# Rank-2 projection of the last pair over 128 rows, and a new order of the first stage, in a gated low-rank feed-forward kernel

## The chip, the cores and the metric

The kernel runs on one core of a Trainium2 chip. The metric is the device time of one execution in microseconds; the time before is 862.0 us, the median of three runs (861.14 to 862.42).

## The reference, cut to what matters

```python
def _qlora_linear(x, wq, A, B):          # wq holds a quarter of the input columns
    w = jnp.tile(wq, (1, 4))
    return x @ w.T + x @ A.T @ B.T * 0.5

def reference(x, w1q, a1, b1, w3q, a3, b3, w2q, a2, b2):     # x: 2 x 2048 x 1024
    xn = layernorm(x)
    s = attn(xn)        # autocorrelation by FFT, its top 6 lags, a softmax over them
    g = silu(_qlora_linear(silu(_qlora_linear(xn, w1q, a1, b1)) * _qlora_linear(xn, w3q, a3, b3),
                           w2q, a2, b2))                     # hidden width 2752, rank 2
    return x + s * g
```

## The kernel before

The 4096 tokens are done in eight groups of 512 (NG = 8), each of four tiles of 128 tokens. The normalised tile is folded to a quarter of its columns, since the weights repeat four times. Each fp32 product with the weights w1 and w3 is made as three fp16 products: the high part of the weights times the high part of x, high times low, and low times high. Hidden columns go by pairs: pair p is 128 columns of w1 (the gate, bank gb[p % 3]) and 128 of w3 (the factor beside it, bank ub[p % 3]). There are 22 pairs (NP_), and the last one (LAST = 21) holds 64 columns of each, side by side.

In a group, TensorE runs `up(i, p)` for each pair (`chain` makes the six products of a bank, L1223; `lora`, L1251, adds the rank-2 part for two pairs at once), ScalarE takes the silu (`gate`), and VectorE multiplies (`product`, L826), which gives h, a ring of six buffers. Every fourth pair TensorE projects four pairs of h onto the rank of a2: `z2(i, n)` (L1365) writes pair p to rows 32 * (p % 4) of the bank zb, so that the four pairs lie in four column strips of the array. The last call, n = 5, holds pairs 20 and 21 alone, and pair 21 reads 64 rows where all others read 128. After it come the second linear layer (`down`, L1424 to L1433, in group 0 `down_high` and `down_low`), the transposes of the next group's x (`xt_across`, L1455), and from group 1 to group 6 `z_across` (L1351), transposes of zs, which VectorE makes by `z_split` (L801) after the first output tile of the group.

All engines work from queues written out by hand, joined by semaphores; nothing is reordered at run time but the loading of weights into the array. The order in the source is the order of the work.

The first stage, before the first pair, differs from the others. SP loads the small a13, the identity, the tiles of x and the weights in four blocks (BLOCK = 0, 4, 10, 16: the first pair of each). TensorE transposes the four tiles (`x_across`, L1440), ScalarE copies them (`x_copy`), TensorE makes the rank-2 projection z0 of x in two halves (`z0`, L1471) and transposes the folded tiles (`quarter_across`, L1446), while POOL computes 1/std and -mean/std (`spread`, L447 to L455) and differences of x (`raw_difference`, L470). Each weight block is scaled by a power of two: ScalarE sums its squares (`w_bound`), TensorE adds them over the rows (`scale_sum`, L1462), VectorE makes the scale (`w_scale`, L1039), ScalarE writes the high part (`w_high`), VectorE the low part (`w_low`, L1059). `z0_spread` (L1478) lays z0 out for `lora`; ScalarE and VectorE split it in three bf16 parts (`z_part`, `z_rest`), beside the same split of b13 (`b_cast`, `b_step`, L1066, `b_scale`). In the pairs of group 0 the rest of this goes on: blocks 1 to 3 of the weights (BOUND_AT, HIGH_AT, LOW_AT), the x tiles of group 1 (`second_x`, L1323 on TensorE and a copy on ScalarE, X_AT = pairs 3, 4, 6, 7, 11, 12, 15, 16), the lags of the autocorrelation (`far_lags`) and the scale sums of blocks 2 and 3 after pair 5. All ScalarE work goes through one helper, so its line is always L526.

Of the kernel before, what the change touches and what calls it, by code (L numbers as in the profile page):

```python
# [9 lines left out]
ALU = mybir.AluOpType  # L10
# [16 lines left out]
NH = 6  # L27
# [24 lines left out]
def pair_rows(p):  # L52
    return P if p < LAST else HALF_ROWS
# [41 lines left out]
def build(nc, d):  # L95
# [3 lines left out]
    with ExitStack() as ctx:  # L99
# [246 lines left out]
        def _(sp):  # L346
# [41 lines left out]
            front_load(0, 2)  # L388
            block_load(0, 1)
            front_load(0, 3)  # L390
# [50 lines left out]
        def _(pool):  # L441
# [14 lines left out]

            def fold(q):
                x = front_buf(0, q)[0]
                pool.wait_ge(xr_loaded[q], 16)
                if q:  # L460
                    pool.wait_ge(fold_done, q)
                tt(yh[:], x[:, 0:HALF], x[:, HALF:L], ALU.add).then_inc(fold_half, 1)
                pool.wait_ge(fold_half, q + 1)
                tt(xq4[:, q, :], yh[:, 0:DQ], yh[:, DQ:HALF], ALU.add).then_inc(fold_done, 1)
# [37 lines left out]
            for q in range(1, 4):  # L502
                spread(0, q)
# [20 lines left out]
        def _(act):  # L524
# [158 lines left out]
            for k in range(4):  # L683
                x_copy(0, k)
            w_bound(0, 1)
            for q in range(3):
                quarter_normal(q)
            x_copy(1, 0)
            x_copy(1, 1)
            quarter_normal(3)  # L690
# [3 lines left out]
            w_high(0, 1)  # L694
            act.wait_ge(rsb_ready, 1)
            A(rsb[:], mb[:], ACT.Copy).then_inc(rsb_done, 1)
            b_cast(0, 0)
# [8 lines left out]
            for i in range(NG):  # L706
                last = i + 1 == NG
                for p in range(NP_):
                    gate(i, p)
                    if i == 0:  # L710
                        for b, m in HIGH_AT.get(p, ()):
                            w_high(b, m)
                        if p in CAST_AT:
                            b_cast(1, CAST_AT[p])
                        if p in B_AT:
                            b_scale(B_AT[p])
                        for b, m in BOUND_AT.get(p, ()):
                            w_bound(b, m)
                        if p in W2_AT:
                            w2_high(W2_AT[p])  # L720
                        if p in X_AT:
                            second_x(2 * X_AT[p][0] + X_AT[p][1])
                    if p in C_AT[i]:
                        square(i, C_AT[i].index(p))
                    if i == 0 and p in FAR0_AT:
                        far_lags(0, FIRST_DIFF[FAR0_AT.index(p)])
                    if not last and p in NORM_AT[i]:
                        normalise(i + 1, NORM_AT[i].index(p))
                    if not last and p in FAR_AT[i]:
                        far_lags(i + 1, FAR_AT[i].index(p))  # L730
                    if p % 4 == 1 and p > 1:
                        folded_high(i, p // 4 - 1)
                    if i == 0 and p == LAST:
                        b2_high()
# [18 lines left out]
        def _(dve):  # L753
# [358 lines left out]
            w_scale(0, 1, mb[:, 0:3])  # L1112
# [95 lines left out]
        def _(pe):  # L1208
# [17 lines left out]
            def first_gate():  # L1226
                for k in range(2):
                    pe.wait_ge(wh_done, 1)
                    pe.wait_ge(xth_done, k + 1)
                    mm(gb[0][:], wt_h[0][:, k, 0:P], xt[:, k, :], start=k == 0, stop=False)  # L1230
                    pe.wait_ge(xtl_done, k + 1)
                    mm(gb[0][:], wt_h[0][:, k, 0:P], xt[:, 2 + k, :], start=False, stop=False)
                    pe.wait_ge(wl_done, k + 1)
                    mm(gb[0][:], wt_l[0][:, k, 0:P], xt[:, k, :], start=False, stop=False)
# [21 lines left out]
            def up(i, p):  # L1256
                bank_free(i, p)
                fresh = i == 0 and p in BLOCK
                if fresh and p:
                    pe.wait_ge(wl_done, 4 * BLOCK.index(p) + 2)  # L1260
                if p % 2 == 0:
                    if i == p == 0:
                        first_gate()
                    else:
                        chain(gb[p % 3], 0, p, True, False)
                    if i == p == 0:
                        z0_spread()
                    if fresh:
                        pe.wait_ge(wl_done, 4 * BLOCK.index(p) + 4)
# [84 lines left out]
            def z2(i, n):  # L1354
# [8 lines left out]
                for p in pairs:  # L1363
                    c, rows = 32 * (p % 4), pair_rows(p)
                    o = mm(zb[c:c + 6, :], a2st[0:rows, p, :], h[0:rows, p % NH, :], start=n == 0, stop=p + 4 >= NP_)  # L1365
# [120 lines left out]
            for q in range(4):  # L1486
                x_across(q)
            pe.wait_ge(zeroed, 9)
            pe.wait_ge(xa_done, 4)
            scale_sum(0, mb, 0)  # L1490
            z0(0)
            for q in range(4):
                quarter_across(q)
            pe.wait_ge(dev_done, 12)
            pe.wait_ge(wall_read, 1)
            for q in range(4):
                o = nc.tensor.transpose(mb[:, q * P:(q + 1) * P], rs[:, q:q + 1].broadcast_to([P, P]), ident[:])
            o.then_inc(rsb_ready, 1)
            pe.wait_ge(xa_done, 6)
            pe.wait_ge(xd_done, 2)  # L1500
            z0(1)
            for i in range(NG):
# [3 lines left out]
                for p in range(NP_):  # L1506
                    up(i, p)
                    if i == 0 and p == 5:
# [3 lines left out]
                    if p % 4 == 1 and 4 < p < NP_ - 1:  # L1512
                        z2(i, p // 4 - 1)
# [88 lines left out]
```

## Time and profile before

| what | value |
|---|---|
| median of three runs | 862.0 us |
| the profiled execution, device time | 861.5 us |
| its span, first to last instruction | 859.7 us |
| TensorE busy (PE) | 841.7 us, 98% of the span |
| VectorE busy (DVE) | 576.4 us, 67% |
| ScalarE busy (ACT) | 331.8 us, 39% |
| GpSimd busy (POOL) | 147.1 us, 17% |
| mean granted TensorE clock | 0.996 of full |

Times in the rows are microseconds from the start of the span. A row of a timeline gives the start, the duration of the merged instructions, the engine (PE a matmul, PEld a weight load), the source line, the operation, the tile written and those read, the shape, the count, and in brackets how long the engine sat idle before it and on whom it waited. One fp32 matmul stands as two instructions. "issue" means that the profile shows nothing it waited for.

### The profile page before, as it was taken

Reading aid. Unit: us, or ns where it says so; the run is one execution under the profiler, and the core shown is the slowest. Engines: PE = TensorE matmul, PEld = TensorE weight load, DVE = VectorE, ACT = ScalarE, POOL = GpSimd, SP = SyncE. Lnnn points to the kernel's source line nnn. Section 1 sums busy time; section 2 is a strip of 40 time slices with the busy share of each in tenths; the row PEclk is TensorE's granted clock in tenths of the full one; section 3 lists DMA queues with packets and bytes.
Section 4 is the critical chain, followed back from the end, with each engine's and each line's share of the span. In section 5 each row is a group of like instructions: output and inputs, shape, how many; then the busy total and the mean of one; then the engine's idle time right before and its main releaser. Section 6 shows DMA issues by size and latency. Waiting matters only on the chain.

```text
span 859.7 us, 11239 instructions
## 1 busy us (share of the span) xinstructions
PE 841.7 (98%) x4200; PEld 441.3 (51%) x4200; DVE 576.4 (67%) x941; ACT 331.8 (39%) x544; POOL 147.1 (17%) x243
## 2 busy tenths in 40 slices
PE   6899999999999999999999999999999999999997
PEld 4334475335744367434664347534475335744366
DVE  6777734686766776688667776678765686744534
ACT  5986635434133342333423332333323334122231
POOL 6042101222012220122101230023201222000000
PEclk8999999999999999999999999999999999999999
DMA  9730026000230003200042010501014000220004
GB/s 290 265 103 25 26 99 221 25 26 24 95 128 26 25 26 123 99 25 25 26 147 74 26 33 18 196 28 47 26 50 172 25 1 0 99 98 1 1 2 146
DMA packets 18903, 62.13 MB, mean 72 GB/s; under 512 B 2464, under 2 KB 4224, under 8 KB 18576
## 3 DMA queue, kind: packets, MB, share of 16 engines
q1 hardware_dynamic: 18832, 61.28, 20.7%
q8 instruction: 33, 0.54, 0.3%
q14 instruction: 38, 0.31, 0.1%
HBM read 44.49 MB, written 16.78 MB: 71 GB/s over the span
## 4 chain that ended last, share of the span: by engine, by line
PE 89%; DVE 4%; ACT 2%; issue 2%; DMA 1%; DVEq 1%; SPq 0%; ACTq 0%
PE g L1223 26%; PE u L1223 24%; PE zb L1365 6%; PE g L1424 4%; PE u L1424 4%; PE u L1433 3%; PE g L1431 3%; PE u L1431 3%; PE g L1433 3%; PE g L1251 3%; DVE junk L783 1%; DMA xf<-in_x 1%; PE mb L1290 1%; PE u L1427 1%; PE g L1427 1%
## 5 line engine op out<-in xcount | busy, mean ns | idle before, releaser
L526 ACT ACTIVATE sil<-g,winv 128x512 f32<-128x512 f32 (+1 forms) x176 | 120.0, 683 | 272.2 <-PE g L1251 244.0
L826 DVE SCALAR_TENSOR_TENSOR h<-u,winv,sil 128x512 f32<-128x512 f32 x168 | 125.7, 749 | 124.0 <-ACT sil L526 109.0
L1223 PE MATMUL u<-xt,w_h 128*128 128x512 f16 x672 | 199.9, 379 | 1.0 <-DVE w_l L1059 1.0
L1223 PE MATMUL g<-xt,w_h 128*128 128x512 f16 x668 | 199.8, 381 | 0.0
L1223 PE MATMUL u<-xt,w_l 128*128 128x512 f16 x336 | 127.3, 379 | 0.0
L1223 PE MATMUL g<-xt,w_l 128*128 128x512 f16 x334 | 126.6, 379 | 0.0
L783 DVE CUSTOM_DVE_ANT_0 junk<-xn,abc 128x1024 bf16<-128x1024 f32 x96 | 120.3, 1253 | 6.0 <-issue 2.7
L1223 PEld LDWEIGHTS u<-xt,w_h 128*128 128x128 f16 x672 | 65.6, 98 | 81.1 <-DVE w_l L1059 2.3
L1223 PEld LDWEIGHTS g<-xt,w_h 128*128 128x128 f16 x668 | 56.6, 98 | 86.1 <-issue 33.8
L447 POOL TENSOR_TENSOR ve<-mv,three 128x1 f32<-128x1 f32 x32 | 6.5, 202 | 475.3 <-DVE mv L765 475.3
L526 ACT ACTIVATE gg<-g 128x512 f32<-128x512 f32 x32 | 19.1, 598 | 148.0 <-PE g L1427 76.1
L977 DVE SCALAR_TENSOR_TENSOR ob<-xr,c_mean,gg 128x1024 f32<-128x1024 f32 x27 | 34.6, 1283 | 60.7 <-ACT gg L526 39.7
L1424 PE MATMUL g<-w_h,hf_h 128*128 128x512 f32 x174 | 72.8, 418 | 0.0
L1424 PE MATMUL u<-w_h,hf_h 128*128 128x512 f32 x174 | 68.8, 396 | 0.0
L1433 PE MATMUL u<-w_h,hf_l 128*128 128x512 f32 x145 | 57.5, 397 | 0.0
L1431 PE MATMUL g<-w_l,hf_h 128*128 128x512 f32 x145 | 57.5, 397 | 0.0
L1365 PE MATMUL zb<-h,a2st 128*6 128x512 f32 (+1 forms) x352 | 57.5, 593 | 0.0
L1431 PE MATMUL u<-w_l,hf_h 128*128 128x512 f32 x145 | 57.4, 396 | 0.0
L1433 PE MATMUL g<-w_h,hf_l 128*128 128x512 f32 x145 | 57.3, 395 | 0.0
L838 DVE TENSOR_TENSOR acc<-acc,h 128x512 f32<-128x512 f32 x80 | 56.2, 703 | 0.0
L1223 PEld LDWEIGHTS u<-xt,w_l 128*128 128x128 f16 x336 | 32.9, 98 | 39.6
L1223 PEld LDWEIGHTS g<-xt,w_l 128*128 128x128 f16 x334 | 32.7, 98 | 39.4
(243 smaller groups left out, 1115.8 us busy)
## 6 DMA issues: line engine op xcount, KB each, us to landing
xr<-in_x SPq DMA_DIRECT2D x32, 512.0 KB, 4.5
out_x<-ob SPq DMA_DIRECT2D x31, 512.0 KB, 2.9
xf<-in_x SPq DMA_DIRECT2D x30, 512.0 KB, 3.3
raw_w<-in_w2t SPq DMA_DIRECT2D x1, 2560.0 KB
abc<-in_a SPq DMA_DIRECT2D x1, 2048.0 KB, 8.1
raw_w<-in_w1t SPq DMA_DIRECT2D x2, 768.0 KB, 8.1
raw_w<-in_w3t SPq DMA_DIRECT2D x2, 768.0 KB, 9.5
raw_w<-in_w1t SPq DMA_DIRECT2D x1, 704.0 KB, 11.7
```

The costliest lines, as they stand in the source:

```text
L526: return nc.scalar.activation(out, in_, f, **kw)
L783: nc.vector.tensor_tensor_reduce(junk[:], xn[:], abc[:, r, :], 1.0, 0.0, ALU.mult, ALU.add, zt[:, q, r:r + 1]).then_inc(z_done, 1)
L826: stt(out=h[0:n, p % NH, :], in0=up, scalar=winv[0:n, 3 * block_of(p) + 1:3 * block_of(p) + 2], in1=sil[0:n, p % 2, :], op0=ALU.mult, op1= ...
L838: o = tt(acc[0:rows, b, :], a, h[0:rows, p % NH, :], ALU.add)
L977: stt(out=o[:], in0=x[:], scalar=c_mean[:, q:q + 1], in1=gg[:], op0=ALU.subtract, op1=ALU.mult)
L1223: o = mm(bank[:], a, x, start=opens and t == 0, stop=closes and t == len(terms) - 1)
L1251: o = mm((gb, ub)[s % 2][k % 3][:], bst[32 * s:32 * s + 32, p // 2, :], zst[32 * s:32 * s + 32, :], start=s >= 2 and not first, stop=s < 2 ...
L1365: o = mm(zb[c:c + 6, :], a2st[0:rows, p, :], h[0:rows, p % NH, :], start=n == 0, stop=p + 4 >= NP_)
L1424: mm(bank[:], hf_h[:, n, t], w2_h[:, n, c:c + 512], start=n == 0, stop=False)
L1427: mm(bank[:], hf_l[:, n, t], w2_l[:, n, c:c + 512], start=False, stop=True).then_inc(dn_ready, 1)
L1431: mm(bank[:], hf_h[:, n, t], w2_l[:, n, c:c + 512], start=False, stop=False)
L1433: mm(bank[:], hf_l[:, n, t], w2_h[:, n, c:c + 512], start=False, stop=False)
```

## The change

Four things are changed.

In z2 pair 21 reads all 128 rows of its weights (rows 64 to 127 are zero) and of h. In the loads, tile 3 of x goes ahead of the w3 part of weight block 0. In the first stage TensorE does the first half of z0 ahead of the fourth tile, the scale sum of block 0 goes to bank gb[0], the last two tiles get 1/std and mean together (`last_spread`), and POOL waits for the low parts of block 0 before its differences. For the first pair of each weight block all products with high weight parts of a bank come ahead of those with low parts (`first_chain`), and in the first pair z0_spread comes ahead of the low parts of the second bank. In group 0, ScalarE copies x tiles of the next group right after `gate`, and z2 comes ahead of the scale sums of blocks 2 and 3.

```diff
@@ loads (SP)
             front_load(0, 2)
+            front_load(0, 3)
             block_load(0, 1)
-            front_load(0, 3)
@@ POOL
+            def last_spread():
+                c = slice(2, 4)
+                pool.wait_ge(stats_done, 4)
+                tt(ve[:, c], mv[:, c, 1], three[:, 0:1].broadcast_to([P, 2]), ALU.add).then_inc(dev_done, 2)
...
+                tt(nm4[:, c], nm[:, c], three[:, 3:4].broadcast_to([P, 2]), ALU.mult).then_inc(nm4_done, 2)
...
-            for q in range(1, 4):
-                spread(0, q)
+            spread(0, 1)
+            last_spread()
+            pool.wait_ge(wl_done, 4)
             for q in FIRST_DIFF:
                 raw_difference(q)
@@ ScalarE
+            quarter_normal(0)
+            quarter_normal(1)
+            x_copy(1, 0)
             w_bound(0, 1)
-            for q in range(3):
-                quarter_normal(q)
-            x_copy(1, 0)
             x_copy(1, 1)
+            quarter_normal(2)
             quarter_normal(3)
             w_high(0, 0)
             xt_high(0, 0)
             xt_high(0, 1)
-            w_high(0, 1)
             act.wait_ge(rsb_ready, 1)
             A(rsb[:], mb[:], ACT.Copy).then_inc(rsb_done, 1)
+            w_high(0, 1)
...
                     gate(i, p)
                     if i == 0:
+                        if p in X_AT:
+                            second_x(2 * X_AT[p][0] + X_AT[p][1])
...
-                        if p in X_AT:
-                            second_x(2 * X_AT[p][0] + X_AT[p][1])
@@ VectorE
-            w_scale(0, 1, mb[:, 0:3])
+            w_scale(0, 1, gb[0][:, 0:3])
@@ TensorE
+            def first_chain(bank, m, p):
+                b, c = BLOCK.index(p), pair_col(p)
+                pe.wait_ge(wh_done, 2 * b + m + 1)
+                for k in range(2):
+                    if p == 0:
+                        pe.wait_ge(xth_done, k + 1)
+                    mm(bank[:], wt_h[m][:, k, c:c + P], xt[:, k, :], start=k == 0, stop=False)
+                for k in range(2):
+                    if p == m == 0:
+                        pe.wait_ge(xtl_done, k + 1)
+                    mm(bank[:], wt_h[m][:, k, c:c + P], xt[:, 2 + k, :], start=False, stop=False)
+                if p == 0 and m:
+                    z0_spread()
+                for k in range(2):
+                    pe.wait_ge(wl_done, 4 * b + 2 * m + k + 1)
+                    mm(bank[:], wt_l[m][:, k, c:c + P], xt[:, k, :], start=False, stop=False)
...
-                    c, rows = 32 * (p % 4), pair_rows(p)
-                    o = mm(zb[c:c + 6, :], a2st[0:rows, p, :], h[0:rows, p % NH, :], start=n == 0, stop=p + 4 >= NP_)
+                    c = 32 * (p % 4)
+                    o = mm(zb[c:c + 6, :], a2st[:, p, :], h[:, p % NH, :], start=n == 0, stop=p + 4 >= NP_)
...
-            for q in range(4):
+            for q in range(3):
                 x_across(q)
+            pe.wait_ge(xa_done, 4)
+            z0(0)
+            x_across(3)
+            for q in range(2):
+                quarter_across(q)
             pe.wait_ge(zeroed, 9)
-            pe.wait_ge(xa_done, 4)
-            scale_sum(0, mb, 0)
-            z0(0)
-            for q in range(4):
-                quarter_across(q)
+            pe.wait_ge(xa_done, 5)
+            scale_sum(0, gb[0], 0)
             pe.wait_ge(dev_done, 12)
-            pe.wait_ge(wall_read, 1)
             for q in range(4):
                 o = nc.tensor.transpose(mb[:, q * P:(q + 1) * P], rs[:, q:q + 1].broadcast_to([P, P]), ident[:])
             o.then_inc(rsb_ready, 1)
+            for q in range(2, 4):
+                quarter_across(q)
...
                     up(i, p)
+                    if p % 4 == 1 and 4 < p < NP_ - 1:
+                        z2(i, p // 4 - 1)
                     if i == 0 and p == 5:
                         pe.wait_ge(x1_done, 2)
                         scale_sum(2, mb, 0)
                         scale_sum(3, mb, 3)
-                    if p % 4 == 1 and 4 < p < NP_ - 1:
-                        z2(i, p // 4 - 1)
```

## Rows read from the trace of the kernel before

**Rows 1.** The page's busy times of the engines over the span.
```profile
PE 841.7 (98%) x4200; PEld 441.3 (51%) x4200; DVE 576.4 (67%) x941; ACT 331.8 (39%) x544; POOL 147.1 (17%) x243
```
**Rows 2.** Stretches, busy by engine, granted PE clock, DMA share, GB/s: 10 to 20 us.
```profile
10.00:20.00 10.00, 7.70 (x55) 5.86 (x59) 7.95 (x18) 8.10 (x16) 9.08 (x21) 0.66 1.11 310
```
**Rows 3.** Timeline of PE, 36 to 40 us: two of its waits in group 0's pairs.
```profile
36.64 0.61 PE L1223 MATMUL u<-xt,w_h 128*128 128x512 f16 x2 [0.79 <-DVE w_l L1059]
...
39.87 0.63 PE L1323 MATMUL mb<-ident,xf 128*128 128x128 f32 x4 [1.75 <-ACT xT L526]
```
**Rows 4.** Timeline of PEld, 97.8 to 102.8 us: the last two z2 of group 0.
```profile
97.84 0.11 PEld L1365 LDWEIGHTS zb<-h,a2st 128*6 128x6 f32 x8 [0.36 <-issue]
98.81 0.19 PEld L1379 LDWEIGHTS g<-w_h,hf_h 128*128 128x128 f32 x1 [0.86 <-issue]
...
100.87 0.09 PEld L1365 LDWEIGHTS zb<-h,a2st 128*6 128x6 f32 x2 [0.36 <-issue]
101.82 0.09 PEld L1365 LDWEIGHTS zb<-h,a2st 64*6 64x6 f32 x2 [0.86 <-issue]
102.77 0.19 PEld L1379 LDWEIGHTS g<-w_h,hf_h 128*128 128x128 f32 x1 [0.86 <-issue]
```
**Rows 5.** Waits, 135 to 860 us: us in total, times, longest.
```profile
ACT xt L526 <- PE u L1455: 4.2, 6, 0.8
PEld mb L1351 <- DVE zs L801: 3.7, 6, 1.3
```
**Rows 6.** Timeline of ACT, 212 to 215 us (group 1).
```profile
212.23 0.60 ACT L526 ACTIVATE zq<-zb 64x512 f32<-64x512 f32 x1
213.59 0.60 ACT L526 ACTIVATE xt<-g 128x512 f16<-128x512 f32 x1 [0.76 <-PE u L1455]
...
214.56 0.62 ACT L526 ACTIVATE zh<-z2f 64x512 fp32r<-64x512 f32 x1
```
**Rows 7.** Timeline of DVE, 225 to 230 us (group 1).
```profile
225.65 1.28 DVE L977 SCALAR_TENSOR_TENSOR ob<-xr,c_mean,gg 128x1024 f32<-128x1024 f32 x1 [3.36 <-issue]
...
229.64 0.70 DVE L801 CAST zs<-zp 128x64 f32<-128x64 bf16 x6
```
**Rows 8.** Timeline of PEld at 230 us: `z_across` of group 1.
```profile
230.40 0.42 PEld L1351 LDWEIGHTS mb<-ident,zs 128*128 128x128 f32 x4 [0.42 <-DVE zs L801]
```
**Rows 9.** Timeline of PE, first stage: fourth tile, both halves of z0, z0_spread.
```profile
13.39 0.69 PE L1440 MATMUL g<-ident,xf 128*128 128x128 f32 x2 [2.17 <-DMA xf<-in_x]
...
15.35 1.93 PE L1471 MATMUL zb<-xT,aT 128*32 128x256 f32 x16
...
19.70 1.07 PE L1471 MATMUL zb<-xT,aT 128*32 128x256 f32 x16
...
22.61 1.13 PE L1478 MATMUL mb<-zc,sel 128*128 128x512 f32 x2 [0.37 <-DVE zc L1121]
```
**Rows 10.** Timeline of ACT, 11 to 41 us.
```profile
11.38 0.61 ACT L526 ACTIVATE xT<-mb 128x512 f32<-128x512 f32 x1
...
17.38 1.13 ACT L526 ACTIVATE w_h<-raw_w,wscl 128x1024 f16<-128x1024 f32 x1
...
23.80 0.60 ACT L526 ACTIVATE z_part<-mb 128x512 bf16<-128x512 f32 x1
...
28.41 1.27 ACT L526 ACTIVATE sil<-g,winv 128x512 f32<-128x512 f32 x2 [0.55 <-PE g L1251]
...
40.85 0.69 ACT L526 ACTIVATE sil<-g,winv 128x512 f32<-128x512 f32 x1 [0.64 <-PE g L1251]
```
**Rows 11.** Timeline of DVE at 60 us: second step of the second b13 half.
```profile
59.95 2.02 DVE L1066 SCALAR_TENSOR_TENSOR bst<-b_part,low,raw_b 128x768 bf16<-128x768 bf16 x1
```
**Rows 12.** Timeline of PE, 62 to 66 us: `lora`, and pair 11 from start to end.
```profile
62.76 0.37 PE L1251 MATMUL g<-zst,bst 32*128 32x512 bf16 x1 [0.27 <-DVE h L826]
...
63.09 0.61 PE L1223 MATMUL g<-xt,w_h 128*128 128x512 f16 x2
...
65.69 0.60 PE L1323 MATMUL mb<-ident,xf 128*128 128x128 f32 x4
```

More of the change, by code:

```diff
@@ L455, in spread @@
                     tt(nm4[:, q:q + 1], nm[:, q:q + 1], three[:, 3:4], ALU.mult).then_inc(nm4_done, 1)
+            def last_spread():
+                c = slice(2, 4)
+                pool.wait_ge(stats_done, 4)
+                tt(ve[:, c], mv[:, c, 1], three[:, 0:1].broadcast_to([P, 2]), ALU.add).then_inc(dev_done, 2)
+                tt(nm[:, c], mv[:, c, 0], three[:, 2:3].broadcast_to([P, 2]), ALU.mult)
+                pool.wait_ge(dev_done, 8)
+                tt(rs[:, c], ve[:, c], three[:, 1:2].broadcast_to([P, 2]), ALU.pow).then_inc(dev_done, 2)
+                pool.wait_ge(dev_done, 10)
+                tt(nm[:, c], nm[:, c], rs[:, c], ALU.mult).then_inc(dev_done, 2)
+                pool.wait_ge(dev_done, 12)
+                tt(nm4[:, c], nm[:, c], three[:, 3:4].broadcast_to([P, 2]), ALU.mult).then_inc(nm4_done, 2)
             def fold(q):
@@ L1224, in chain @@
                 return o
-            def first_gate():
+            def first_chain(bank, m, p):
+                b, c = BLOCK.index(p), pair_col(p)
+                pe.wait_ge(wh_done, 2 * b + m + 1)
                 for k in range(2):
[L1228 to L1234, printed above, removed]
+                    if p == 0:
[10 more added lines that the diff above has]
+                    mm(bank[:], wt_l[m][:, k, c:c + P], xt[:, k, :], start=False, stop=False)
             def bank_free(i, p):
@@ L1258, in up @@
                 fresh = i == 0 and p in BLOCK
[L1259 to L1269, printed above, removed]
+                if fresh:
+                    first_chain(gb[p % 3], 0, p)
+                    first_chain(ub[p % 3], 1, p)
+                elif p % 2 == 0:
+                    chain(gb[p % 3], 0, p, True, False)
                     chain(ub[p % 3], 1, p, True, False)
```

## The prediction

> **What bounds the kernel now.** I read the busy times first: TensorE is busy 98% of the span, VectorE 67%, ScalarE 39% [rows 1]. So nearly any microsecond taken off TensorE's own queue comes off the time, unless something it waits for arrives no earlier. Next I read the stretches. From 20 us on TensorE has its full clock; from 10 to 20 us it is busy only 7.7 of 10 us, at a mean granted clock of 0.66, which is a mixture of its two levels, 1.2 and 2.4 GHz [rows 2]. The same 16 instructions of half a z0 take 1.93 us at 15.35 and 1.07 us at 19.70 [rows 9]. Then TensorE's waits: in the pairs of group 0 the largest are 0.79 us for low weights and 1.75 us for a copy of x [rows 3]. After pair 11 starts, at 62.76, I find hardly any, except ahead of z_across [rows 5, 12]. Last I read the weight loads of z2, since its last call looked too long for half the work.
>
> **z2, eight times.** The reader should see the starts in [rows 4]. A call with four pairs of 128 rows loads all its weights at once and is over when the next load starts: 98.81 - 97.84 = 0.97 us. The call with two pairs loads pair 20 at 100.87, sits 0.86 us, and loads pair 21, which has 64 rows, only at 101.82; the next work starts at 102.77. That is 1.90 us for half the pairs. Four column strips of equal height run side by side; the strip of another height waited for the array to empty. With 128 rows pair 21 is like pair 20, and the nearest row for two equal strips is that of four, so I take 0.97 us. Saved: 0.93 us a call, 7.44 us for eight. The zero rows cost nothing, since a matmul's time in these rows goes by its 512 columns. The bounds: nothing saved (two equal strips run one after the other) and 0.93.
>
> The row shows the second load held until the first matmuls were over. The Trainium skill ("TensorEngine Tiling (Array Packing)", Key Properties) says that a change of tiling mode drains the engine; the trace agrees, with its 0.95 us between the two loads. The Trainium skill also has a rule against this change: "TensorE: Matmul & The Clock Gate", Part 3, says that a weight load overlaps a running matmul only if its row group differs. Pairs 20 and 21 would share all row groups, so by that rule nothing is gained here; the eight loads of four such pairs that start together at 97.84 speak against it.
>
> **What of it reaches the end.** In groups 0 and 7 no z_across follows and TensorE has no wait behind z2: 2 x 0.93 = 1.86 us. In groups 1 to 6 z_across waits for zs. Its load starts at 230.40, 0.06 us after VectorE's zs ends (229.64 + 0.70 = 230.34), and the weight load had sat 0.42 us [rows 7, 8]; all six did so, 3.7 us in total [rows 5]. So there is no slack: the gain is what VectorE's chain moves. Followed back it is zs, an output tile from 225.65 (after 3.36 us in which the flag is read and the branch taken), four projections, xt_low, hf_l, which needs ScalarE's zh at 214.56, which is queued behind xt at 213.59, which waited 0.76 us for TensorE's transposes [rows 6, 7]. Those come 0.93 us earlier, but ScalarE is busy with zq until 212.83, and zq is behind work that does not move. So this chain moves by the wait, 4.2 us in six groups, 0.70 each [rows 5], or some 0.1 more as the next copy may start before the last has ended. zh would start at 213.8, and z2f, which VectorE makes between zq and zh, then has 1 us since zq's end at 212.83, so nothing new is late. I take 0.75: 6 x 0.75 = 4.5 us. What is lost is given back as 0.2 us more of waiting per z_across. Sum of z2: 6.4 us, bounds 5.9 and 7.4.
>
> **The first stage.** The fourth tile lets TensorE start at 13.39 after sitting 2.17 us [rows 9]. It is now ahead of a load of the same 512 KB, so I estimate that it lands some 1.9 us earlier, near 11.4, and the w3 part near 13.4. The new queue first waits for the four copies of the first half, the last at 11.38 + 0.61 = 11.99 [rows 10], then runs z0(0) and the tile. At full clock z0(0) ends at 13.0 and the tile near 13.9; at the low clock near 13.9 and 15.6, against some 15.2 before. ScalarE has x_copy(1, 0) ahead of w_bound(0, 1), so a late tile now holds the weights as well: behind that wait are w_bound, the scale, two quarter_normal and w_high. Full clock: w_high(0, 0) starts at 17.05 instead of 17.38 [rows 10]; low clock: near 18.2. Merging the two spreads takes about five POOL instructions off and makes rs ready some 1 us earlier, but quarter 2 later; both are hidden by w_bound.
>
> Then the order of the first pair counts. z0_spread starts at 22.61 now, and second-bank products follow it [rows 9]. In the new order four high products of the second bank come first, and rsb is copied ahead of w_high(0, 1), so zc is ready about 1 us earlier. At full clock the spread starts near 22.0; if the clock is low through the gate products, near 23.1. ScalarE's z_part, now at 23.80, starts at 23.05 or 24.1. From it hang z_rest, z_part again, w_bound(1, 1), b_scale and lora. ScalarE is dense to its gate at 28.41: it moves by about 0.95 earlier or 0.15 later.
>
> POOL's new wait for the low parts has its four differences, the copies of a2 and a memset queued behind it. The copies wait for a load until 30 anyway. SP's load of group 1's tile 0 waits for the first difference and is issued near 23.7 instead of 19.8; the queues are full of weights until later, so I cost it at nothing; if that cover fails, second_x is late by up to the shift. The differences leave VectorE's w_low and fall on its b_step and z_rest. The nearest row is a step of the same kind that lasted 2.02 us while POOL was busy too [rows 11]; I price POOL's share at nothing to half of it, 0 to 1.0 us, and take 0.3, as the steps here are shorter.
>
> ScalarE then runs without a gap until the wait of 0.64 us at 40.85, which comes of TensorE's 1.75 us wait for an x copy queued behind two w_bound [rows 3, 10]. With the copy right after `gate` both waits vanish, but since ScalarE bounds this stretch only its 0.64 us comes off. The 0.79 us for low weights [rows 3] goes too and is worth nothing for the same reason. z2 ahead of the scale sums gives TensorE about one more microsecond (one call of 0.97 us), but the chain of scale sum, w_high, product, w_low and b_step to b_scale(2), which pair 11's lora awaits with just 0.27 us in hand [rows 12], moves only with the scale sum. So TensorE gets at most 0.3 us of that.
>
> Sum: 0.95 - 0.3 + 0.64 = 1.3 us with the full clock, -0.15 - 0.3 + 0.64 = 0.2 us with the low one. Rows 2 show that the clock fell in this very stage, and the new order has more gaps after 14 us, so I hold both about equally likely and take 0.8 us. Bounds: a loss of 0.9 (low clock, late weights, full POOL price) and a gain of 2.6 (nothing of POOL, and the one microsecond reaches lora).
>
> Against the profiled execution's own 861.5 us: 861.5 - 6.4 - 0.8 = 854.3 us. It lies 0.5 below the median of 862.0, inside the runs' scatter, so the forecast is 854.4 us.
>
> **The rivals.** (1) Equal strips of two pairs don't run side by side, or the full-height form keeps the old 1.90 us: only the first stage counts, 861.5 - 0.8 = 860.7. For it: no row shows a call with two equal strips. Against: four do. (2) The wait on zs takes the place of z2's time: if VectorE's chain doesn't move (zh comes no earlier, or the flag read sets it), groups 1 to 6 give nothing, 861.5 - 1.86 - 0.8 = 858.8. Against: ScalarE visibly waited for TensorE. (3) Slower: the cut-up work of the first stage makes the clock fall and it stays low. A pair costs 65.69 - 63.09 = 2.6 us at full clock [rows 12] and would cost 5.2; low until pair 3 is over, the gate products and three pairs cost some 1.7 + 3 x 2.6 = 9.5 us, less 1 for slack: 861.5 - 6.4 + 8.5 = 863.6. It decides from the third slow pair on. Against: once the pairs run, TensorE has work without a gap, and it kept its clock through the waits of rows 3. (4) More from the first stage than its bounds, with lora moving by 3 us or more: below 851.6.
>
> **How the numbers follow.** Forecast case 0.82; (1) 0.05; (2) 0.06; (3) 0.04; (4) 0.03. The case's own range is 861.5 - 7.4 - 2.6 = 851.5 to 862.0 - 5.9 + 0.9 = 857.0, and it alone holds the wanted 8 in 10, so the range is 851.5 to 857.0. Within 0.2% (1.7 us, about what a measurement of this kernel can tell from no change) falls rival 1: 0.05. Slower is 0.04, faster 0.91.
>
> **What would show it.** Right: in z2's last call four weight loads start together and the next starts 0.97 us on, in all eight groups; z_across waits about 0.2 us longer each; gate 0 starts near 27.8, and lora of pair 11 near 62. Wrong: two separate loads 0.95 us apart (rival 1); xt no earlier against the start of its group (rival 2); a granted clock of 0.5 after 24 us (rival 3); w_high(0, 0) later than 18.5 would put the first stage in its bad half.

## The result, and the profile after

| kernel | median, us | runs | ratio to before, 95% interval |
|---|---|---|---|
| before | 861.7 | 861.14 to 862.42 | |
| after | 855.05 | 854.57 to 855.45 | 0.9922 [0.9905, 0.9939] |

The change saves 6.6 us. The forecast was 854.4 in a range of 851.5 to 857.0. The profiled execution of after took 854.57 us, its span 852.8; it stands against 861.5 and 859.7 before.

First the busy times of the page, beside [rows 1]. TensorE has 8.7 us less to do, of which 7.5 is z2 (its group of rows: 57.5 us before, 50.0 after). The share of 98% stays: what bounded the kernel still does.

```profile
PE 833.0 (98%) x4200; PEld 439.7 (52%) x4200; DVE 576.9 (68%) x941; ACT 331.6 (39%) x544; POOL 148.0 (17%) x238
```

The timeline of the weight loads at the same place as [rows 4], the last two z2 of group 0:

```profile
96.75 0.12 PEld L1382 LDWEIGHTS zb<-h,a2st 128*6 128x6 f32 x8 [0.36 <-issue]
97.73 0.19 PEld L1396 LDWEIGHTS g<-w_h,hf_h 128*128 128x128 f32 x1 [0.86 <-issue]
...
99.78 0.10 PEld L1382 LDWEIGHTS zb<-h,a2st 128*6 128x6 f32 x4 [0.36 <-issue]
100.74 0.19 PEld L1396 LDWEIGHTS g<-w_h,hf_h 128*128 128x128 f32 x1 [0.86 <-issue]
```

The last call has one group of four loads instead of two groups of two, and the next work loads 0.96 us later instead of 1.90. The call with twice the pairs still takes 0.98. So two strips of 128 rows cost what four do.

Next ScalarE, VectorE and the weight load of `z_across` in group 1, where the recorded numbers of before are [rows 6 to 8]:

```profile
210.20 0.60 ACT L540 ACTIVATE zq<-zb 64x512 f32<-64x512 f32 x1
210.82 0.60 ACT L540 ACTIVATE xt<-g 128x512 f16<-128x512 f32 x1
...
211.79 0.62 ACT L540 ACTIVATE zh<-z2f 64x512 fp32r<-64x512 f32 x1
```
```profile
222.90 1.28 DVE L992 SCALAR_TENSOR_TENSOR ob<-xr,c_mean,gg 128x1024 f32<-128x1024 f32 x1 [3.38 <-issue]
...
226.87 0.70 DVE L816 CAST zs<-zp 128x64 f32<-128x64 bf16 x6
```
```profile
227.63 0.42 PEld L1368 LDWEIGHTS mb<-ident,zs 128*128 128x128 f32 x4 [0.61 <-DVE zs L816]
```

The copy xt no longer waits for the transposes. Between the starts of zq and zh lie 1.59 us; before it was 214.56 - 212.23 = 2.33. That 0.74 is all the chain moved, and it reached zs unchanged. TensorE's load now sits 0.61 us instead of 0.42. The waits from 130 us to the end show the same for all six groups (us in total, times, longest):

```profile
PEld mb L1368 <- DVE zs L816: 5.3, 6, 1.4
PE mb L1368 <- DVE zs L816: 2.5, 5, 1.0
```

Before, these were 3.7 [rows 5] and 1.2 us. So the loads sit 1.6 us longer over the six groups, or 0.27 each, and the matmuls 1.3, or 0.22 each; which of the two is lost time is settled below. The row of xt waiting for u, 4.2 us before, is gone. From the last z2 of one group to that of the next, groups 1 to 7, it is (825.18 - 207.71) / 6 = 102.91 us before and (819.16 - 205.68) / 6 = 102.25 after: 0.66 less, which is 0.93 less 0.27. Group 1 is one of the better ones; from group 2 to group 3 only 0.27 us is gained, since VectorE's chain moved by less there and the load sits 1.04 instead of 0.39.

Now the first stage. TensorE, 12 to 24 us, against [rows 9]:

```profile
12.07 1.07 PE L1488 MATMUL zb<-xT,aT 128*32 128x256 f32 x16 [0.78 <-ACT xT L540]
13.08 0.44 PE L1457 MATMUL g<-ident,xf 128*128 128x128 f32 x2
...
15.99 0.16 PE L1479 MATMUL g<-wsum,ones_h 128*128 128x2 bf16 x1 [1.38 <-ACT w_sq L540]
...
16.51 0.65 PE L1515 MATMUL mb<-ident,rs 128*128 128x128 f32 x4 [0.31 <-POOL nm L466]
...
18.59 1.94 PE L1488 MATMUL zb<-xT,aT 128*32 128x256 f32 x16
...
22.75 1.02 PE L1495 MATMUL mb<-zc,sel 128*128 128x512 f32 x2
```

The tile's transposes start at 13.08 with no wait for a transfer; it sat 2.17 us before. But the work ahead of the first pair is now cut up by waits for ScalarE (1.38, the squares of w3) and POOL (0.31), and the stretches (columns as in [rows 2]; the number before the last two is the granted clock) show what follows:

```profile
14.00:16.00 2.00, 0.62 (x7) 0.41 (x6) 1.32 (x3) 1.82 (x5) 1.58 (x3) 1.00 1.24 209
16.00:18.00 2.00, 1.37 (x10) 0.84 (x10) 1.52 (x6) 1.50 (x4) 0.51 (x3) 0.76 1.00 310
18.00:20.00 2.00, 2.00 (x19) 0.86 (x18) 1.34 (x3) 2.00 (x4) 0.00 (x0) 0.50 1.02 394
20.00:22.00 2.00, 2.00 (x15) 0.67 (x8) 2.00 (x4) 2.00 (x4) 0.00 (x0) 0.89 1.05 412
```

The clock is at its lower level from somewhere past 16 to past 20 us, and the second half of z0 takes 1.94 us. ScalarE and POOL in this stage:

```profile
16.83 1.09 ACT L540 ACTIVATE xq<-xq,nm,rs 128x256 f32<-128x256 f32 x2 [0.50 <-POOL nm L468]
17.82 1.13 ACT L540 ACTIVATE w_h<-raw_w,wscl 128x1024 f16<-128x1024 f32 x1
...
23.81 0.60 ACT L540 ACTIVATE z_part<-mb 128x512 bf16<-128x512 f32 x1 [0.27 <-PE mb L1495]
...
28.26 1.27 ACT L540 ACTIVATE sil<-g,winv 128x512 f32<-128x512 f32 x2 [0.55 <-PE g L1274]
```
```profile
14.42 0.69 POOL L461 TENSOR_TENSOR ve<-mv,three 128x2 f32<-128x2 f32 x1 [1.03 <-DVE mv L780]
...
15.26 0.86 POOL L464 TENSOR_TENSOR rs<-ve,three 128x2 f32<-128x2 f32 x1
...
16.60 0.19 POOL L468 TENSOR_TENSOR nm<-nm,three 128x2 f32<-128x2 f32 x1
```

w_high(0, 0) starts at 17.82, later than the 17.38 of before, and z_part at 23.81, as before (23.80) [rows 10]. ScalarE waits 0.50 us for POOL's merged spread. Last, TensorE's waits from the first `lora` to that of pair 11, both included:

```profile
27.86 0.37 PE L1274 MATMUL g<-zst,bst 32*128 32x512 bf16 x1 [0.26 <-ACT bst L540]
...
43.27 0.18 PE L1479 MATMUL mb<-wsum,ones_h 128*128 128x2 bf16 x1 [1.68 <-ACT w_sq L540]
...
61.68 0.37 PE L1274 MATMUL g<-zst,bst 32*128 32x512 bf16 x1 [1.52 <-DVE h L841]
```

The waits of [rows 3] are gone. Two of 1.68 and 1.52 us are new: TensorE runs ahead of the others and sits for the scale sum of block 3 and at pair 11's `lora` instead (there VectorE's h ends at 61.55 and ScalarE's bst at 61.53; which of the two holds it the trace can't tell). The latter starts 1.08 us earlier than in [rows 12]. From there to the end of the span it is 852.8 - 61.68 = 791.1 us, before 859.7 - 62.76 = 796.9. So in the profiled pair 1.1 us came ahead of pair 11 and 5.8 behind it, where all eight last calls of z2 lie.

### The profile page after: what moved, and what is told of

Read it like the earlier page. It is cut to its first block, busy times and chain, and to the rows that moved or that the text cites. A ratio compares the mean times of both kernels' runs of the same rounds, so it can differ in the third digit from the quotient of the medians.

```text
span 852.8 us, 11238 instructions
## 1 busy us (share of the span) xinstructions
PE 833.0 (98%) x4200; PEld 439.7 (52%) x4200; DVE 576.9 (68%) x941; ACT 331.6 (39%) x544; POOL 148.0 (17%) x238
## 4 chain that ended last, share of the span: by engine, by line
PE 69%; DVE 14%; ACT 6%; issue 6%; DVEq 3%; POOL 1%; DMA 1%; SPq 0%; ACTq 0%; POOLq 0%
PE g L1238 23%; PE u L1238 22%; PE zb L1382 4%; DVE junk L798 4%; PE g L1274 3%; PE g L1441 2%; PE u L1441 2%; PE u L1450 2%; PE g L1448 2%; PE u L1448 2%; PE g L1450 2%; DVEq L857 1%; ACT sil L540 1%; DVE h L841 1%; DVEq L779 1%
## 5 line engine op out<-in xcount | busy, mean ns | idle before, releaser
L1238 PE MATMUL g<-xt,w_h 128*128 128x512 f16 x656 | 196.3, 381 | 0.0
L1238 PE MATMUL u<-xt,w_h 128*128 128x512 f16 x656 | 195.2, 379 | 0.0
L1238 PE MATMUL g<-xt,w_l 128*128 128x512 f16 x328 | 124.4, 379 | 0.0
L1238 PE MATMUL u<-xt,w_l 128*128 128x512 f16 x328 | 124.4, 379 | 0.0
L1448 PE MATMUL u<-w_l,hf_h 128*128 128x512 f32 x145 | 57.5, 397 | 0.0
L1382 PE MATMUL zb<-h,a2st 128*6 128x512 f32 x352 | 50.0, 593 | 0.0
```

Of the source, the lines that this page charges most:

```text
L1238: o = mm(bank[:], a, x, start=opens and t == 0, stop=closes and t == len(terms) - 1)
L1382: o = mm(zb[c:c + 6, :], a2st[:, p, :], h[:, p % NH, :], start=n == 0, stop=p + 4 >= NP_)
L1448: mm(bank[:], hf_h[:, n, t], w2_l[:, n, c:c + 512], start=False, stop=False)
```

## Experiments

Each median is of 4 to 11 executions, timed beside the kernel before (861.45 to 861.58 us each time); z2_both64 was executed once. Differences of 0.4 to 0.6 us between variants of the changed kernel are no larger than the spread of their executions (0.3 to 1.3 us), so where such a difference is read below, it is the profile that carries it.

**z2 by itself.** The kernel before with:

```diff
-                    c, rows = 32 * (p % 4), pair_rows(p)
-                    o = mm(zb[c:c + 6, :], a2st[0:rows, p, :], h[0:rows, p % NH, :], ...)
+                    c = 32 * (p % 4)
+                    o = mm(zb[c:c + 6, :], a2st[:, p, :], h[:, p % NH, :], ...)
```

> The kernel before with one edit: pair 21 reads 128 rows in z2. Theory (the last z2 call falls from 1.90 to 0.96 us, and VectorE's chain to zs gives some of it back in groups 1 to 6): 5.5 to 6.4 us less than before, TensorE's waits for zs in z_across near 2.5 us in total instead of 1.2. Rival (the whole gain of the change but a little comes from the first stage): under 4 us less. Rival (all of the eight savings of 0.94 us reach the end): 7.5 us less, waits for zs unchanged.

Measured: 856.93 us (855.19 to 858.14), ratio 0.9943 [0.9930, 0.9957]. That is 4.6 us, less than the 5.5 to 6.4 expected and more than the rival's 4; but the five runs scattered over 3 us, and the fastest two gave 6.4. So it was timed again:

> The kernel before with pair 21 on 128 rows in z2, as z2_only, whose five executions lay 3 us apart in two or three heaps (855.2, 857.0, 858.1) with mean granted clocks of 0.999, 0.995 and 0.997. Theory (TensorE's wait of 1.7 us before pair 5 lets the clock fall in some executions, which costs 1.5 to 3 us; the early copy of the change takes the wait away): again two heaps 1.5 us or more apart, the lower near 855.2. Rival (the first five were a scatter by chance): one heap, about as narrow as that of the changed kernel.

Measured: 855.36 us (855.07 to 855.84), ratio 0.9928 [0.9914, 0.9941], 6.1 us under the 861.45 of the kernel before beside it. The two heaps of the theory did not come back. The median of all ten executions is 855.4, again 6.1 us less. In the first five the mean granted clock was 0.999 in the two runs at 855.2, and 0.995 to 0.997 in the three at 856.9 to 858.1; where in the kernel the clock was missing I can't say, as the profiled one was among the fast.

**The rest by itself.** The changed kernel with the old z2:

```diff
-                    c = 32 * (p % 4)
-                    o = mm(zb[c:c + 6, :], a2st[:, p, :], h[:, p % NH, :], ...)
+                    c, rows = 32 * (p % 4), pair_rows(p)
+                    o = mm(zb[c:c + 6, :], a2st[0:rows, p, :], h[0:rows, p % NH, :], ...)
```

> The changed kernel with the old z2 (64 rows for pair 21): the first stage's new order alone. Theory (the first stage is worth what lora of pair 11 moved, 1.1 us): 0.7 to 1.4 us less than before, and z2_only and this one add up to the whole change within 0.5 us. Rival (the two parts share a gain or clash): the sum is off by over 1 us.

Measured: 861.12 us (860.38 to 861.56), ratio 0.9994 [0.9985, 1.0003]. The first stage and the order in group 0 give 0.4 us, at most 1.3 by the interval: less than the 0.7 to 1.4 expected. The two parts add up, 6.1 + 0.4 against 6.6, with z2's part taken from all ten executions; with the first five alone it would be 5.0. The profile of this run also shows z2's price a second way: it has the same group 0 as after up to pair 11 (61.64 and 61.68), and its span is 858.8 us against 852.8, 6.0 more.

**Equal height or full height?** The kernel before with both pairs of the last call at 64 rows:

```diff
-                    c, rows = 32 * (p % 4), pair_rows(p)
+                    c, rows = 32 * (p % 4), P if p < LAST - 1 else HALF_ROWS
```

> The kernel before, but pairs 20 and 21 both read 64 rows in z2; this leaves out rows 64 to 127 of pair 20 in the projection onto a2, as a measurement. Theory (what held the second strip back was its height against the first one's, whatever the height): the last z2 call loads all its weights at once and takes about 0.96 us, and the time is near that of z2_only. Rival (only strips of full height run side by side): two loads about 0.95 us apart, 1.90 us for the call, and the time of before.

Measured: 855.47 us, one execution. TensorE's timeline at the last z2 of group 0:

```profile
100.51 1.03 PE L1365 MATMUL zb<-h,a2st 64*6 64x512 f32 x4
101.46 0.50 PE L1379 MATMUL g<-w_h,hf_h 128*128 128x512 f32 x1
```

The next matmul follows after 0.95 us, where two strips of 128 rows take 0.96. It is the difference in height between the strips that costs, not the low height.

**Does VectorE's chain to zs bound what z2 can give?** The changed kernel, with two of the four projections ahead of zs put into gaps in which VectorE waits for zq and zh (0.85 and 0.93 us in group 1 of after):

```diff
             def last_projections(i):
-                for r in range(4):
+                for r in range(2, 4):
                     project(i, 3, r)
@@ z2_stack
+                if i and i + 1 < NG:
+                    project(i + 1, 3, 0)
                 dve.wait_ge(zq_done, i + 1)
...
+                if i and i + 1 < NG:
+                    project(i + 1, 3, 1)
                 dve.wait_ge(zh2_done, i + 1)
```

> The changed kernel, where VectorE makes the first of the last four projections before it waits for zq and the second before it waits for zh, in place of after xt_low. Theory (in groups 1 to 6 z_across waits for VectorE's chain, and that chain idles about 1.8 us for ScalarE): zs ends 1.5 to 2.5 us earlier, TensorE's waits for zs go from 2.5 us to under 0.5 us, and the kernel is 1.5 to 2.5 us faster than the changed one. Rival (what sets zs is the flag read and the output tile, which depend on other things): no change.

Measured: 851.02 us (850.56 to 851.51), ratio 0.9878 [0.9863, 0.9893]: 4.0 us under after, where I had expected 1.5 to 2.5. VectorE and the load of `z_across` in group 1:

```profile
221.14 1.29 DVE L996 SCALAR_TENSOR_TENSOR ob<-xr,c_mean,gg 128x1024 f32<-128x1024 f32 x1 [3.42 <-issue]
...
225.13 0.70 DVE L816 CAST zs<-zp 128x64 f32<-128x64 bf16 x6
```
```profile
227.10 0.59 PEld L1372 LDWEIGHTS mb<-ident,zs 128*128 128x128 f32 x4
```

zs is done at 225.83, 1.3 us before TensorE gets there, and no wait for zs is left in any group. From one last z2 to the next it is 101.57 us in all of the six. In after it is more, and by how much follows from what the load of `z_across` sat (us):

| groups of after | 1 to 2 | 2 to 3 | 3 to 4 | 4 to 5 | 5 to 6 | 6 to 7 |
|---|---|---|---|---|---|---|
| the load sat | 0.61 | 1.04 | 1.40 | 0.96 | 0.58 | 0.68 |
| last z2 to last z2 | 101.98 | 102.41 | 102.77 | 102.33 | 101.95 | 102.05 |

Each is 101.57 plus the load's wait less 0.20, and their excess adds up to 4.0 us. Before, the same holds with 102.50, that is 0.93 more. The matmul's recorded waits for zs had been 2.5 us only. What they leave out is the lead of the load: in proj_early the load starts at 227.10 and its matmul at 227.33, while in after both start at 227.63, so the lead of 0.23 us is lost whenever the load sits. So the bound of groups 1 to 6 was VectorE, as rival 2 had it, though that rival's price (nothing gained in these groups) was wrong, because the chain itself moved.

**Is the early copy of x what helps in group 0?** The changed kernel with `second_x` back behind the weight work:

```diff
                     if i == 0:
-                        if p in X_AT:
-                            second_x(2 * X_AT[p][0] + X_AT[p][1])
...
+                        if p in X_AT:
+                            second_x(2 * X_AT[p][0] + X_AT[p][1])
                     if p in C_AT[i]:
```

> The changed kernel, but ScalarE copies the x tiles of group 1 in their old place, after the other work of the pair. Theory (the early copy removes the wait of 0.64 us on ScalarE before gate 4, and nothing else of it counts): TensorE waits again 1.5 to 2 us for the copy before pair 5, lora of pair 11 starts 0.5 to 0.7 us later than in the changed kernel, and the time is 0.4 to 0.8 us longer than the changed one's. Rival (the first stage's gain comes from the first pair alone): within 0.2 us of the changed kernel.

Measured: 857.78 us (856.29 to 858.05), ratio 0.9951 [0.9937, 0.9964], so 2.7 us slower than after (1.2 for the fastest execution), far beyond both expectations. TensorE waits longer than in [rows 3], and then its clock falls:

```profile
39.54 0.63 PE L1340 MATMUL mb<-ident,xf 128*128 128x128 f32 x4 [2.72 <-ACT xT L540]
...
41.16 1.06 PE L1238 MATMUL g<-xt,w_h 128*128 128x512 f16 x2
```
```profile
40.00:41.00 1.00, 1.00 (x9) 0.41 (x8) 0.00 (x0) 0.48 (x1) 0.40 (x2) 1.00 1.05 451
41.00:42.00 1.00, 1.00 (x4) 0.30 (x2) 0.76 (x2) 1.00 (x3) 0.00 (x0) 0.50 1.27 541
...
43.00:44.00 1.00, 1.00 (x4) 0.33 (x3) 0.00 (x0) 1.00 (x4) 0.00 (x0) 0.50 0.82 348
44.00:45.00 1.00, 1.00 (x7) 0.27 (x9) 0.00 (x0) 0.85 (x3) 0.00 (x0) 0.79 1.12 299
```

Two products that take 0.59 us take 1.06. Pair 5 lasts 44.81 - 40.43 = 4.4 us against 2.6 [rows 12], which is 1.8 us. And since z2 now stands ahead of the scale sums, block 2's scale comes later as well. `lora` of pair 11 starts at 64.39, 2.7 us later than in after. The medians lie 2.7 apart too, the profiled executions 3.5 (858.05 and 854.57); the rest of the 3.5 comes in groups 1 to 6. Whether the clock fell there in the other four executions is not known. To part the copy from the order, the same copy was put into a kernel with the old order (the kernel before with the rows of z2 changed):

```diff
                     if i == 0:
+                        if p in X_AT:
+                            second_x(2 * X_AT[p][0] + X_AT[p][1])
...
-                        if p in X_AT:
-                            second_x(2 * X_AT[p][0] + X_AT[p][1])
```

> The kernel before with two edits: pair 21 reads 128 rows in z2, and ScalarE copies the x tiles of group 1 right after the gate. Nothing else of the change. Theory (of the first stage's edits only the early copy counts, with what it spares TensorE: the wait before pair 5 and the clock's fall that follows it in some executions): within 0.5 us of the changed kernel, and its executions lie within 1.2 us of each other. Rival (the order of the first pair and the loads bring the rest): 0.6 us or more slower than the changed kernel.

Measured: 855.43 us (855.03 to 856.70), ratio 0.9927 [0.9913, 0.9940], the same as z2_only_again. The profiled run was the slowest, and TensorE shows why:

```profile
43.97 0.18 PE L1462 MATMUL mb<-wsum,ones_h 128*128 128x2 bf16 x1 [1.78 <-ACT w_sq L526]
...
45.22 1.03 PE L1223 MATMUL g<-xt,w_h 128*128 128x512 f16 x2
```

The wait of 1.75 us in [rows 3] is gone here; one as long stands at the scale sums instead, and the clock fell after it (0.73 in 44 to 46 us, 0.50 in 46 to 48). The median is within the 0.5 us of after that was expected, but the executions lie 1.7 us apart, not 1.2, and against z2_only_again the median gains nothing from the copy alone.

The profiles up to the scale sum of block 3 part the two all the same. Counted from the first `lora`, that sum starts 44.26 - 28.00 = 16.26 us in before, 43.27 - 27.86 = 15.41 in after, and 43.97 - 28.56 = 15.41 in z2_x_copy. So the early copy alone moves it by 0.85 us, and z2 ahead of the sums adds nothing. Behind that point z2_x_copy loses it again to the low clock: pair 6 and the z2 before it last 49.34 - 44.13 = 5.2 us, against 0.97 + 2.6 [rows 4, 12].

The clock was at full from 22 us to near the end in the seven profiles that have both the copy and the order, and in the four that have neither (before, z2_only, z2_only_again, z2_both64). It fell in the two that have one of them, one profile each. That is too few to say that the combination decides it: a pause of 1.75 us stands in before and one of 1.68 in after (at 43.27), and why these are harmless is not shown.

**POOL's wait for the low parts.** The changed kernel without it (the differences then run beside VectorE's w_low):

```diff
             last_spread()
-            pool.wait_ge(wl_done, 4)
             for q in FIRST_DIFF:
```

> The changed kernel without POOL's wait for the low parts of block 0: its four differences start at about 16.8 instead of 23.6. Theory (beside POOL, VectorE's steps of z and b13 cost 0.3 us, and the wait trades that for 0.16 us on w_low): 0 to 0.4 us faster than the changed kernel, with the b_step at 25 us back to 0.88 us. Rival (the differences cost w_low and the second half of the copies of x more): 0.2 to 0.6 us slower.

Measured: 855.43 us (854.95 to 856.26), ratio 0.9932 [0.9918, 0.9946]; 0.4 slower than after, as the rival had it, though inside the scatter. Its first `lora` starts at 28.42 instead of 27.86; 0.28 of the 0.56 was already there at the scale sum (16.27 instead of 15.99), ahead of the wait in question. The other 0.28 is VectorE beside POOL's differences: one step of the scale took 0.70 us instead of 0.17, and the first w_low, which starts at 19.21 (after: 18.99), took 1.09 instead of 0.75. So by this pair of profiles the wait is worth some 0.3 us.

**Did the low clock of the first stage hold anything?** The changed kernel with 26 transposes of the identity (11 + 3 + 2 x 3 + 6; the expectation says 29) into bank zb, results that nothing reads, in TensorE's idle time:

```diff
+            def fill(n):
+                for k in range(n):
+                    nc.tensor.transpose(zb[:, 256 + P * (k % 2):384 + P * (k % 2)], ident[:], ident[:])
...
+            fill(11)
             pe.wait_ge(zeroed, 9)
             pe.wait_ge(xa_done, 5)
             scale_sum(0, gb[0], 0)
+            fill(3)
...
             for q in range(2, 4):
+                fill(3)
                 quarter_across(q)
+            fill(6)
```

> The changed kernel with 29 extra transposes of the identity into an unused half of the bank zb, put where TensorE waits between 14.4 and 18.5 us; nothing reads them. Theory (TensorE's clock falls to its low level near 16 us as the engine is idle before it, and that is what keeps z_part at 23.8): the clock stays full from 16 to 19.4 us, z0(1) takes 1.0 instead of 1.94 us, z_part starts 0.3 to 0.7 us earlier and the kernel is 0.2 to 0.7 us faster. Rival (ScalarE bounds the stage, not the clock): within 0.2 us of the changed kernel, whatever the clock.

Measured: 854.44 us (854.31 to 854.62), ratio 0.9917 [0.9904, 0.9931].

```profile
18.96 1.07 PE L1488 MATMUL zb<-xT,aT 128*32 128x256 f32 x16
```
```profile
23.72 0.60 ACT L540 ACTIVATE z_part<-mb 128x512 bf16<-128x512 f32 x1 [0.28 <-PE mb L1499]
```

The clock is full in all of 14 to 22 us and z0(1) takes 1.07 us, but z_part starts only 0.09 earlier than in after. The clock was low in after and cost next to nothing there, as the rival had it. The time is nevertheless in the theory's range: the 0.6 us between the medians is more than the profiles explain (`lora` of pair 11 at 61.60 against 61.68, and both spans 852.8).

**Did the merged spread cost the 0.5 us that ScalarE waits?** The changed kernel with the spreads apart again:

```diff
-            spread(0, 1)
-            last_spread()
+            for q in range(1, 4):
+                spread(0, q)
```

> The changed kernel, but POOL makes 1/std and mean of tiles 2 and 3 one after the other, as before the change, in place of both at once. Theory (in the changed kernel ScalarE waits 0.50 us at 16.8 for the merged result, and w_high(0, 0) starts at 17.8 for that; split, quarter 2 is ready early): w_high(0, 0) starts 0.2 to 0.6 us earlier, gate 0 and lora of pair 11 move by as much, and the kernel is 0.2 to 0.6 us faster than the changed one. Rival (the rest of the chain to z_part, through zc, holds it): within 0.2 us.

Measured: 854.42 us (854.12 to 855.15), ratio 0.9920 [0.9906, 0.9934].

```profile
16.23 1.08 ACT L540 ACTIVATE xq<-xq,nm,rs 128x256 f32<-128x256 f32 x2
17.21 1.14 ACT L540 ACTIVATE w_h<-raw_w,wscl 128x1024 f16<-128x1024 f32 x1
```

The wait of 0.50 us is gone, all that follows on ScalarE comes 0.6 us earlier (z_part 23.20, the first silu 27.66), pair 11's `lora` at 61.09 instead of 61.68, and the median fell by 0.6.

**All of it together:** proj_early, fill and spread_split in one kernel.

> The changed kernel with three edits: two of the last four projections in VectorE's gaps, the unused transposes that keep TensorE's clock up from 14.4 to 18.5 us, and POOL's results of tiles 2 and 3 one after the other. Theory (the projections give 4.0 us, as alone, since z_across no longer waits; with w_high earlier the clock is no longer idle either): 850.3 to 851.0 us. Rival (the two first-stage edits are worth nothing with the rest): 851.0 us or more, as with the early projections alone.

Measured: 850.06 us (849.98 to 850.65), ratio 0.9868 [0.9853, 0.9884]. That is 11.4 us under before and 5.0 under after, slightly better than the 850.3 to 851.0 expected. Its `lora` of pair 11 starts at 61.16, no earlier than in spread_split: fill adds nothing measurable to the split.

## Why the prediction was right, point by point

**z2: 7.44 us off TensorE, 6.4 to the end.** Right. The last call takes 0.96 us (predicted 0.97); alone it gave 6.1 us. The chain to zs moved 0.74 in group 1 (0.75), but less in others: the six groups gained 0.66 us each on average, 4.0 in all, where I had 4.5. The 0.2 us "given back" per group came out as 0.27, the longer wait of the load; I had taken all six groups to be like the first. With 0.93 or 0.94 from each of groups 0 and 7 the profiled pair gained 5.85 us. The two strips ran side by side, so rival 1 falls. The Trainium skill's remark that a change of tiling mode drains the engine ("TensorEngine Tiling (Array Packing)", Key Properties) agrees with z2_both64: with no change of height between the strips there is no drain, at 64 rows either. The rule by which a weight load overlaps a running matmul only if its row group differs (the Trainium skill, "TensorE: Matmul & The Clock Gate", Part 3) is not what the trace shows: the four loads, all of 128 rows, lie within 0.10 us from 99.78, while the first matmul of the call runs from 99.78 to 100.38.

**The first stage: 0.8 us, bounds -0.9 to 2.6.** Measured 0.4, interval -0.3 to 1.3, so inside; but the terms were not what I had said, and that their errors cancel is luck. The low side of the bounds, a loss of 0.9, is not worked out in the prediction: its named terms give at most 0.5.

- The weights. I took w_high(0, 0) at 17.05 with the full clock and 18.2 with the low one. It came at 17.82, and the clock had no part in it: stage_only has the same code with z0(1) in 1.07 us and starts w_high at 17.79. The step that failed is "quarter 2 later ... both hidden by w_bound". POOL's merged spread starts only when the last tile's statistics are there and ends at 16.79; ScalarE had nothing left to do 0.50 us before. spread_split measured the term at 0.6 us. Nor was rs ready 1 us earlier: POOL's power for the last tiles ended at 16.12, before at 16.30.
- The start of `lora`. I took ScalarE's dense part as 0.95 earlier or 0.15 later. The kernels that share before's first stage start the first `lora` at 28.00 (before), 27.41 (z2_only), 27.57 (z2_only_again), 27.62 (z2_both64) and 28.56 (z2_x_copy), mean 27.8. Those with after's first stage start it at 27.86, 27.82, 27.68, 27.77 and 27.91 (after, stage_only, x_copy_late, fill, proj_early), mean 27.8. So the new order gained nothing here on average; it only made the time steadier, 0.2 us apart instead of 1.2. In four of the first five the `lora` comes 13.95 to 13.98 us behind the start of the fourth tile's transposes (13.46, 13.61, 13.64 and 14.59), so there the late tile decides. In before it comes 14.61 behind (13.39): the granted clock was 0.50 from 14 to 18 us, and ScalarE waited for TensorE's transposes ahead of xt, which it does not in z2_only, where the clock was full:

```profile
19.22 0.60 ACT L526 ACTIVATE xt<-g 128x512 f16<-128x512 f32 x1 [0.70 <-PE u L1446]
```
```profile
18.48 0.57 ACT L526 ACTIVATE xt<-g 128x512 f16<-128x512 f32 x1
```

So the low clock cost some 0.65 us in the profile that I forecast from. In z2_both64 (old order, 0.50 in 14 to 17 us) and in after it was low for about half as long and cost nothing. The late tile no longer shows in the new order: its transposes start at 13.03 to 13.09 in all five. I had seen the clock as a danger of the new order only.

- From the first `lora` to that of pair 11 it is 34.76 us in before, 34.77 in both z2_only kernels, and 33.82 in after and stage_only. That is 0.94 us, and the only real gain ahead of the groups. I had 0.64 for it from the copy and up to 0.3 from z2 ahead of the sums, and had then taken the sum at 0.8 for other reasons. Of the 0.94, 0.85 is there at the scale sum of block 3 and comes of the copy alone (above). z2 ahead of the sums is not what gained. Without the early copy the new order has 36.7 us for this stretch (x_copy_late, 64.39 - 27.68), 1.8 of it from the low clock in pair 5; with the old order the early copy alone has 35.2 (z2_x_copy, 63.71 - 28.56), also with a low clock in it.
- The price of POOL's wait, 0.3. VectorE's steps did get slower beside POOL (1.15 and 1.21 us at 25.12 and 26.20, where pool_free has 0.88 and 0.74), but ScalarE was dense there, so nothing of it reached `lora`. The term was 0, and the wait gained some 0.3 by sparing w_low, which I had not counted.

The profiles thus say 0.9 for the first stage against kernels of the old kind, the medians 0.3 to 0.4. The profiled executions of after and stage_only are 0.5 and 0.6 us under their medians, and those of before and z2_only_again within 0.2 of theirs, which accounts for the difference. What makes the other executions of the new order slower is not shown.

**The rivals.** Rival 3 (the clock stays low) did not occur in after: from 22 us on the clock was full. But x_copy_late shows its mechanism in the middle of the pairs, and so my argument against it, that TensorE kept its clock through the waits of [rows 3], was too weak: it rested on one execution with a wait of 1.75 us. Rival 2 was the nearest miss. The bound was there, and proj_early took 4 us from it, but it moved with z2. Rival 4 asked for 3 us from the first stage; nothing near that was there.

## What to carry to other kernels

Give the column strips of one TensorE pass the same number of rows, even if half of them are zeros: here a strip of another height was loaded only 0.95 us after the first, and equal height gave 6.1 of the 6.6 us. When work is taken off the bounding engine, read where it next waits, and whether the chain behind that wait holds gaps into which something can be moved; here that was worth 4 us beside the 6 of the change. And compare a stage over several executions before a gain in it is counted: the spread between profiles of the same first stage, 1.2 us, was larger than what the change did to it, and the one that the forecast was made from had a cost of its own in it.

## What the runs showed of the hardware that was not expected

- A pause of 1.8 or 2.7 us between dense matmuls was followed, in one profile each, by some 3 us at the 1.2 GHz level (x_copy_late: 0.50 from 41 to 44 us after 2.72 us; z2_x_copy: products at 45.22 in 1.03 us instead of 0.59 after 1.78 us). Pauses of 1.75 us in before and z2_only and of 1.68 in after were not. The fall came 1.0 and 1.5 us after work had started again, not in the pause; in the first stage of before it came within the pause of 2.17 us (1.00 in 12.0 to 12.5 us, 0.53 in 12.5 to 13.0). How often it comes, and what decides it, is open.
- In the first stage the same 16 instructions of z0(1) took 1.94 us in after and 1.07 in stage_only, with the same code up to there; the start of the first `lora` differed by 0.04 us.
- A load that sits for its input costs more than the wait that the matmul shows: 5.3 us on the load, 2.5 on the matmul, and 4.0 gained by removing both. In each of six groups the cost is the load's wait less 0.20 us, since the load's lead of 0.23 on its matmul is lost.
- Merging POOL's operations on two single columns into one on both did not pay on this chain: the power takes 0.86 us for two columns (L464) and 0.55 for one in spread_split. The merged chain lasts 16.79 - 14.42 = 2.37 us from the last tile's statistics, that of one tile 16.44 - 14.62 = 1.82, and in the merged one tile 2's result waits for tile 3's.
